# A two-layer graph kernel: the first layer's order written out for each engine by itself, x loaded between the weight slices

## What is computed

```python
h = relu(layernorm(x))                       # x: 1024 x 512, float32
q, k, v = h @ Wq + bq, h @ Wk + bk, h @ Wv + bv
adj = zeros(1024, 1024); adj[src, dst] = 1   # 33,792 edges, sorted by dst
a = q @ k.T / sqrt(512) * adj + (1 - adj) * -1e6
x = x + softmax(a) @ v
h = relu(layernorm(x))
agg = segment_sum(h[src], dst) / max(degree, 1)
out = x + alpha * (agg @ W.T + b)
```

## Time and profile before

| | us |
|---|---|
| median of 3 runs (lowest, highest) | 252.75 (252.17, 253.19) |
| the profiled execution | 252.01 |
| its span, first to last instruction | 250.2 |
| TensorE, VectorE, ScalarE, GpSimd busy | 237.3, 169.9, 79.3, 66.9 |
| mean granted TensorE clock | 0.986 of full |

### The profile page before, as it was taken

The page is one execution under the profiler, slowest core; times in us unless marked ns, Lnnn a source line. Parts: engine busy times, 40 slices in busy tenths (PEclk is TensorE's granted clock), DMA queues, the critical chain, the costliest instruction groups (busy, mean ns, idle before and its releaser), DMA issues.

```text
span 250.2 us, 3366 instructions
## 1 busy us (share of the span) xinstructions
PE 237.3 (95%) x1296; PEld 190.4 (76%) x1296; DVE 169.9 (68%) x352; ACT 79.3 (32%) x139; POOL 66.9 (27%) x102
## 2 busy tenths in 40 slices
PE   7998399949999999999999999999999999999995
PEld 5464388747888887878888888888888888888885
DVE  6998967897999998169584998585856153145322
ACT  2058808834322223013236054141603202041000
POOL 4044312300000000299643156070414503200000
PEclk9999859999999999999999999999999999999999
DMA  6990000000010000100400000000000000001222
GB/s 200 326 355 6 0 0 4 0 0 0 3 42 1 3 0 3 42 1 4 149 19 0 3 0 0 0 3 0 0 0 3 0 0 0 4 3 42 84 102 108
DMA packets 5617, 9.42 MB, mean 38 GB/s; under 512 B 864, under 2 KB 1376, under 8 KB 5600
## 3 DMA queue, kind: packets, MB, share of 16 engines
q1 hardware_dynamic: 4880, 8.91, 10.1%
q10 hardware_dynamic: 720, 0.28, 0.4%
HBM read 7.09 MB, written 2.10 MB: 37 GB/s over the span
## 4 chain that ended last, share of the span: by engine, by line
PE 64%; issue 24%; DVE 4%; ACT 3%; POOL 2%; DMA 2%; SPq 0%; DVEq 0%; POOLq 0%
PE bank L848 14%; PE bank L849 14%; PE bank L850 14%; PE bank L992 12%; PE bank L905 3%; PE bank L1012 3%; PE bank L869 2%; DMA wk_raw<-in_wkT 2%; PE bank L915 1%; DVE g_terms L632 1%; PE bank L929 1%; POOL b_sb L417 1%; DVE ohW L594 1%; ACT h L473 1%; DVE pr L773 1%
## 5 line engine op out<-in xcount | busy, mean ns | idle before, releaser
L594 DVE TENSOR_TENSOR ohW<-iotaW,key_b 128x640 bf16<-128x640 bf16 (+4 forms) x66 | 29.9, 453 | 0.0
L590 DVE TENSOR_TENSOR ohL<-iotaL,lo_b 128x512 bf16<-128x512 bf16 x66 | 27.4, 416 | 1.5 <-issue 1.5
L848 PE MATMUL bank<-V_hi,pT_hi 128*128 128x512 f32 x64 | 25.5, 399 | 0.0
L848 PE MATMUL bank<-hT_hi,GT_hi 128*128 128x512 f32 x64 | 25.0, 391 | 0.0
L849 PE MATMUL bank<-V_lo,pT_hi 128*128 128x512 f32 x64 | 24.9, 390 | 0.0
L850 PE MATMUL bank<-V_hi,pT_lo 128*128 128x512 f32 x64 | 24.9, 390 | 0.0
L850 PE MATMUL bank<-hT_hi,GT_lo 128*128 128x512 f32 x64 | 24.9, 389 | 0.0
L849 PE MATMUL bank<-hT_lo,GT_hi 128*128 128x512 f32 x64 | 24.9, 389 | 0.0
L992 PE MATMUL bank<-A,h_hi 128*128 128x512 f32 x64 | 24.9, 389 | 0.0
L992 PE MATMUL bank<-A,h_lo 128*128 128x512 f32 x64 | 24.9, 389 | 0.0
L869 PE MATMUL bank<-ohW,ohL 128*128 128x160 bf16 (+17 forms) x334 | 23.1, 219 | 0.7 <-DVE ohW L594 0.5
(11 more groups left out here) (135 smaller groups left out, 521.9 us busy)
## 6 DMA issues: line engine op xcount, KB each, us to landing
xs<-in_x SPq DMA_DIRECT2D x4, 512.0 KB, 9.3
out_dram<-o_sb SPq DMA_DIRECT2D x7, 256.0 KB, 2.0
wq_raw<-in_wqT SPq DMA_DIRECT2D x4, 256.0 KB, 5.5
wk_raw<-in_wkT SPq DMA_DIRECT2D x4, 256.0 KB, 6.4
wv_raw<-in_wv SPq DMA_DIRECT2D x1, 1024.0 KB, 11.7
wt_raw<-in_wT SPq DMA_DIRECT2D x1, 1024.0 KB, 5.3
bv_sb<-in_bv SPq DMA_DIRECT2D x1, 256.0 KB, 3.2
b_sb<-in_b SPq DMA_DIRECT2D x1, 256.0 KB, 3.0
```

The source lines that it names most:

```text
L590: nc.vector.tensor_tensor(ohL[:, q % RING, :, :].rearrange("p b (m two) -> p b m two", two=2), bcast(iotaL[:, :].rearrange("p (m two) -> p ...
L594: nc.vector.tensor_tensor(ohW[:, q % RING, :, 0:row].rearrange("p b (m two) -> p b m two", two=2), bcast(iotaW[:, 0:row].rearrange("p (m t ...
L848: mm(out, lhs[0][a], rhs[0][b], start=(first and k == 0), stop=False)
```

## The change

- `PLAN` and the code that makes lists from it go. Three orders stand in their place, one for each engine: `PE_ORDER`, `ACT_ORDER`, `DVE_ORDER`. `cN` is N batches of counts, `oN` N batches of one-hots, `kN` the copy of group N into A, `sq` is `squares`, `dot` is `csum`. GpSimd follows ScalarE's `sum` and `sq`.
- `stats` goes: ScalarE makes the statistics of all eight tiles.
- SP issues the first half of x (tiles 0 to 3) between weight slices 1 and 2.
- `g` leaves the rotation of the banks (it goes to bank 7, with semaphores `g_ps` and `g_kept`), so `PROJ` has 21 entries and V7 has index 20 instead of 21.
- `bb` is a step of its own, on TensorE and VectorE.
- G4's low part waits for `u_sum`, V waits for its tile's `hT_lo`, and SP's load of bv no longer waits for `proj_hi`.

```diff
-PLAN = [(("Mk", 0), [], [], 0),
-        (("Mk", 1), [], [], 5),
-        (("M", 0), ["stats 0", "stats 1"], [], 2),
...
-        (("V", 6), [], [], NB),
-        (("V", 7), [], [], 0)]
+PE_ORDER = ("Mk0 bb Mk1 c4 M0 c3 M1 c2 T0 c2 M2 T1 c2 T2 M3 T3 c5 G0 c1 T4 g G1 c3 T5 T6 c6 G2 T7 G3 c3 G4 G5 c4 G6 u c4 V0 "
+           "c4 V1 c3 G7 c6 V2 c4 V3 c4 V4 V5 c2 V6 V7 c4")
+ACT_ORDER = ("sum0 sum1 sum2 sq0 sum3 sq1 sq2 rows0 rows1 k0 M0 sq3 sum4 M1 T0 rows2 sum5 k1 M2 T1 rows3 T2 k2 M3 T3 sq4 k3 "
+           "sum6 sq5 sum7 rows4 rows5 T4 wv0 sq6 rows6 k4 T5 sq7 G0 T6 G1 rows7 k5 G2 wv1 T7 G3 k6 G4 k7 G5 k8 G6 u k9 V0 "
+           "V1 k10 G7 k11 V2 k12 V3 V4 k13 V5 V6 k14 k15 V7")
+DVE_ORDER = ("o12 bb M0 o2 M1 o1 T0 o2 T1 M2 T2 o1 M3 T3 o1 gsum o2 g T4 o8 T5 T6 o1 wv0 o3 T7 G0 G1 G2 o2 wv1 G3 usum o2 G4 "
+           "o2 G5 o2 G6 o2 dot0 o3 dot1 o2 dot2 o2 u o2 dot3 o4 V0 o1 V1 o3 G7 dot4 o2 dot5 o1 dot6 o1 V2 o1 V3 o1 V4 V5 "
+           "V6 dot7 V7")
...
+PROJ = [s for s in PE_STEPS if s[0] in ("M", "u", "G", "V")]
...
             for k in range(KD):
+                if k == 2:
+                    rows_in(0)
+                    rows_in(1)
                 for raw, w_d, loaded in ((wq_raw, wqT_d, ld_wq), (wk_raw, wkT_d, ld_wk)):
                     sp.dma_start(raw[:, k, :], w_d[k * P:(k + 1) * P, :]).then_inc(loaded[k], 16)
...
+            rows_in(2)
+            rows_in(3)
...
                         if n == 0:
-                            act.wait_ge(proj_lo, proj_index(("g", 0)) + 1)
+                            act.wait_ge(g_kept, 1)
...
+                        if n == KD:
+                            dve.wait_ge(u_sum, 1)
...
+                elif step == "bb":
+                    pe.wait_ge(vec_ready, 1)
+                    mm(bank[7][:, 0:KD + 1], f(ones_r[:, :]), bprod[:, :], start=True, stop=True).then_inc(bb_ps, 1)
+                elif step == "g":
+                    pe.wait_ge(g_sum, 1)
+                    pe.wait_ge(hT_lo, KD)
+                    for m in range(KD):
+                        last = mm(bank[7][:, m:m + 1], t_g[:, m * P:(m + 1) * P], f(ones_r[:, 0:1]), start=True, stop=True)
+                    last.then_inc(g_ps, 1)
...
+                        pe.wait_ge(hT_lo, n + 1)
```

More of the change, by code:

```diff
@@ L85 @@
 LAST = {g: max(t for t in range(ET) if any(p[0] == g for p in pieces(t))) for g in range(NG)}
-PLAN = [(("Mk", 0), [], [], 0),
[22 rows of a table removed]
-        (("V", 6), [], [], NB),
-        (("V", 7), [], [], 0)]
-STATS0 = sum(s.startswith("stats") for _, others, _, _ in PLAN for s in others)
-WARM = 8
[L124 to L147, removed]
@@ new lines, with steps @@
+WARM = 8
+def steps(order):
+    out, at = [], 0
+    for step in order.split():
+        what = step.rstrip("0123456789")
+        n = int(step[len(what):] or 0)
+        if what in ("c", "o"):
+            out.append(("count", at, at + n))
+            at += n
+        else:
+            out.append((what, n))
+    assert at in (0, NB)
+    return out
+PE_STEPS, ACT_STEPS, DVE_STEPS = steps(PE_ORDER), steps(ACT_ORDER), steps(DVE_ORDER)
+PROJ = [s for s in PE_STEPS if s[0] in ("M", "u", "G", "V")]
@@ L394, in norm1 @@
             def norm1(layer, t):
-                pool.wait_ge(stats, layer * STATS0 + t + 1)
+                pool.wait_ge(stats, t + 1)
                 link(nc.gpsimd.tensor_scalar(var_e[:, layer, t:t + 1], mv[:, t, 1:2], EPS, None, ALU.add))
@@ L407, in _ @@
             pool.wait_ge(consts, 5)
[L408 to L411, removed]
+            for step, n in ACT_STEPS:
+                if step == "sum":
                     minus_mean(n)
-                elif step == "squares":
+                elif step == "sq":
                     norm0(n)
@@ L460, in norm_relu @@
                                      scale=rstd[:, layer, t:t + 1]).then_inc(relu, 1)
[L462 to L467, removed]
+            act.wait_ge(consts, 2)
+            nc.scalar.activation(iotaL[:, :], iota_i[:, 0:P], ACT.Copy).then_inc(tables, 1)
+            nc.scalar.activation(iotaW[:, :], iota_i[:, 0:NT * WIN], ACT.Copy, bias=1.0).then_inc(tables, 1)
+            for step, n in ACT_STEPS:
+                if step == "sum":
                     if n % 2 == 0:
@@ L470, in _ @@
                     nc.scalar.activation(h1[:, n, :], xs[:, n, :], ACT.Copy, accum_out=xsum[:, n:n + 1]).then_inc(summed, 1)
-                elif step == "squares":
-                    act.wait_ge(centred, n + 1 - STATS0)
+                elif step == "sq":
+                    act.wait_ge(centred, n + 1 )
                     nc.scalar.activation(h1[:, n, :], xs[:, n, :], ACT.Square, bias=nmean[:, n:n + 1],
@@ L485, in _ @@
                                          ACT.Copy).then_inc(hT_hi, 1)
[L486 to L492, removed]
+                elif step == "k":
+                    act.wait_ge(oh_used, LAST[n] // BATCH + 1)
+                    nc.scalar.activation(A[:, :, n * GRP:(n + 1) * GRP], bank[n % 2][:, :].rearrange("p (h d) -> p h d", h=NT),
+                                         ACT.Copy).then_inc(count_kept, 1)
                 elif step in ("M", "u", "G", "V"):
@@ L611, in split_lo @@
                 nc.vector.tensor_tensor(hl[1][:, :, :], raw[:, :, :], f(hl[0][:, :, :]), ALU.subtract).then_inc(w_lo, 1)
[L613 to L625, removed]
+            edge_keys()
+            dve.wait_ge(ld_bqk, 32)
+            link(nc.vector.tensor_scalar(bqk_s[:, :, :], bqk[:, :, :], SCALE, None, ALU.mult))
+            nc.vector.tensor_tensor(bprod[:, 0:KD], bqk_s[:, 0, :], bqk[:, 1, :], ALU.mult).then_inc(vec_ready, 1)
+            for step, n, *to in DVE_STEPS:
+                if step == "count":
+                    one_hots(n, to[0])
+                elif step == "bb":
+                    dve.wait_ge(bb_ps, 1)
+                    nc.vector.tensor_scalar(flag[:, :], bank[7][:, KD:KD + 1], float(P), None, ALU.is_lt).then_inc(flag_ready, 1)
+                    nc.vector.tensor_scalar(windowed[:, :], bank[7][:, KD:KD + 1], float(P), None, ALU.is_ge)
+                    nc.vector.tensor_reduce(bb[:, :], bank[7][:, 0:KD], AX.X, ALU.add).then_inc(bb_kept, 1)
                 elif step in ("gsum", "usum"):
@@ L649, in _ @@
                 elif step == "g":
-                    i = proj_index((step, n))
-                    dve.wait_ge(proj, i + 1)
-                    nc.vector.tensor_copy(g0[:, :], bank[2 + i % 4][:, 0:KD]).then_inc(proj_lo, 1)
+                    dve.wait_ge(g_ps, 1)
+                    nc.vector.tensor_copy(g0[:, :], bank[7][:, 0:KD]).then_inc(g_kept, 1)
                 elif step == "u":
                     i = proj_index((step, n))
-                    dve.wait_ge(proj_hi, hi_before(i + 1))
+                    dve.wait_ge(proj_hi, i + 1)
                     nc.vector.memset(dbad[:, :], 0.0).then_inc(proj_lo, 1)
-                elif step == "csum":
+                elif step == "dot":
                     dve.wait_ge(relu, n + 1)
-                    dve.wait_ge(proj_hi, hi_before(proj_index(("u", 0)) + 1))
+                    dve.wait_ge(proj_hi, proj_index(("u", 0)) + 1)
                     if n >= 2:
@@ L883, in cols @@
                 return (every, k, slice(m * width, (m + 1) * width))
-            for step, n, *to in STEPS:
+            for step, n, *to in PE_STEPS:
                 if step == "count":
                     count(n, to[0])
+                elif step == "bb":
+                    pe.wait_ge(vec_ready, 1)
[6 more added lines that the diff above has]
+                    last.then_inc(g_ps, 1)
                 elif step == "T":
@@ L917, in _ @@
                     last.then_inc(proj, 1)
-                elif step in ("u", "g", "G", "V"):
+                elif step in ("u", "G", "V"):
                     i = proj_index((step, n))
@@ L925, in _ @@
                         last = mm(ps[:, :], f(ones_r[:, :]), t_u, start=True, stop=True)
-                    elif step == "g":
-                        pe.wait_ge(g_sum, 1)
-                        for m in range(KD):
-                            last = mm(ps[:, m:m + 1], t_g[:, m * P:(m + 1) * P], f(ones_r[:, 0:1]), start=True, stop=True)
                     elif step == "G":
```

26 lines of the change are left out of this document (8 added, 18 removed), and 20 rows, old and new, of the table PLAN.

## The result

| | before | changed |
|---|---|---|
| median, 4 runs each (lowest, highest), us | 252.46 (251.96, 253.19) | 244.61 (243.59, 245.41) |
| ratio, 95% interval | | 0.969 (0.964 to 0.973) |
| the profiled execution, us | 252.01 | 245.40 |
| its span, us | 250.2 | 243.6 |
| mean granted TensorE clock in it | 0.986 | 0.993 |

The forecast was 244.3 us. The four runs of the changed kernel come in two kinds: two took 245.40 and 245.41 (span 243.6, clock 0.993), two 243.81 and 243.59 (spans 242.0 and 241.8, clock 0.999 and 1.000).

A forecast was written before the change was run, and what follows sets the result against it. TensorE's waits and slowed clock in the first layer's front were the time to win, with VectorE nearly full. G0 at 28.1 plus 65.0 put `scores(0)` at 93.1 against 101.47, −8.4 us: forecast 244.3 us, range 242.3 to 247.3.

The forecast's parts named there:

- the layout's own 243.6: Whole kernel: time expected for an execution like the profiled 252.01 us one, after −8.4 us, before adding 0.74 us.
- The start: `bb` between `Mk0` and `Mk1`: new TensorE wait of 1.1 us, `Mk1` from 9.8, VectorE waiting about 1 us at `o5`.
- Term 1: Front up to G0: VectorE sets G0, which starts at 28.1 instead of 32.91 us; −4.8 us.
- ScalarE's statistics at no cost: Before T0: 2.6 us added on ScalarE, seven statistics and two normalisations done by 15; cost nothing, cover 4 us.
- The loads: x ahead of weight slices 2 and 3: slice 3 lands near 12.5, M0 wants it at 14.3; hidden, 1.8 us spare.
- Term 2: G0 to `scores(0)`, 68.56 us before: clock and waits gained, `g`, one-hot waits and a V7 wait added; −3.55 us.
- The stretch behind: Behind `scores(0)`: nothing changes, the old length of 148.7 us stays within 0.3.
- a clock of 1.00 throughout the first layer: Sign to look for: TensorE's granted clock at 1.00 in the whole first layer; 0.5 in the front would refute.
- the rival that I gave 0.13: TensorE's clock falls at a remaining stall, costing about 2.7 us, so 247.0 us; chance 0.13.
- loads: Start of the kernel: bias loads and slice 3 may slip by 2 us under x's load, about 245.8 us; chance 0.10.
- VectorE as a bound by 3.5 us: VectorE, without a gap, holds TensorE at most counts: 5% more on 70 us, 247.8 us; chance 0.06.
- slower: Slice 3 queues behind everything, M0 blocks the counts and the clock falls; landing at 22 gives 254.7 us; chance 0.03.

The follow-up runs named there:

- all three repairs: Changed kernel with V7 copied out before the last two groups of counts, `bb` behind `Mk1` and tile 6's squares earlier; 241.20 us, ratio 0.953.
- the first experiment: Changed kernel with ScalarE copying V7 out before the last two groups of counts (V7 k14 k15); 242.33 us, ratio 0.959.
- VectorE work: Changed kernel with two bn_stats and two bn_aggr, results unused, put back on VectorE behind the seventh one-hot pair; 246.01 us, ratio 0.973.

## Why the prediction was right

The time lay 0.3 us from the forecast, and the mechanism was in the main the forecast one. That the distance is so small is partly luck: no run took 244.6 us. The two runs at full clock took 243.81 and 243.59, which is the layout's own 243.6, without the 0.74 us that I added because the old median lay above the old profiled run; the fall of the clock in the other two, which I had left to a rival, lifted the median by about as much. By the steps of the prediction:

- **The start.** `bb` starts at 9.73 and `Mk1` at 9.98 (forecast 9.8), `o5` waits 1.04 us for the first count (forecast about 1). The run with `bb` late shows that this costs 0.84 us up to the end. The trace puts only 0.53 us down as idle in front of `bb`, while the distance from start to start gives 9.73 − 5.12 − 3.55 = 1.06. In this profile one of the 16 records of `Mk0` and `Mk1` is missing, as in that of x late, which shows 0.63. The five other profiles with `bb` early show 0.93 to 0.95 us at this place, and that with the 0.13 that the overlap hides is the distance.
- **Term 1, −4.8 us to G0.** Measured −4.69 (28.22 for 28.1), with `hT_lo` as the releaser and 0.75 us of TensorE idle (forecast 0.8). Its parts are shown one by one, counted from `bprod`: `gsum` 2.76, the statistics on ScalarE 1.58, x's place 2.06, and `bb` −0.84. They don't add up to 4.69, and need not: each was undone alone in the new order.
- **ScalarE's statistics at no cost.** Right with x early, though the seven statistics and two normalisations end at 16.2 and not by 15: the first copy of A behind them, at 16.60, still waited 0.40 us for TensorE. But the cover was judged by the wrong waiter. I named T0, 4 us away. The run with x late moved the statistics by 3.4 us and G0 by 2.1, through the copy of A that stands behind them.
- **The loads.** M0 didn't wait, and VectorE didn't wait for the small loads of the biases (bq's took 4.8 us for 4.3 before). x landed for a first sum at 9.87, at the late end of my 8 to 10, and the sum of tile 2, from the second load, started at 11.24. In the run of all three repairs M0 did wait, so the 1.8 us that I had to spare are not safe once TensorE comes earlier.
- **Term 2, −3.55 us.** The stretch from G0 to `scores(0)` took 65.13 us, forecast 65.0. That is luck in part, as two entries in it were wrong and nearly cancelled: I had 0.7 us of TensorE waiting for one-hots, and the trace has none; and I took T6's old wait of 0.26 off, and the trace has one of 1.07 us. The row of tile 6 waits for three operations of GpSimd behind its squares, and one of them took 1.29 us where 0.19 is its short value; the prediction gives them no length. Why no matmul waits for one-hots stays open: the wait for tile 6 didn't remove those waits, for the run with its squares early has neither. The new wait in front of `scores(0)` was 1.90 us, forecast 2.05, and its larger cause was the forecast one: the first experiment removed 1.25 of it by ScalarE's order alone.
- **The stretch behind** was forecast at 148.7 within 0.3 us. Without a fall of the clock it is 148.55 to 148.64, by the six profiles that have none there; with one it is 150.25, so in the profiled run this sign failed, and so did the one of a clock of 1.00 throughout the first layer. This is the rival that I gave 0.13: it is half true, as two of four runs have it. I priced it at 2.7 us, from the old fall; measured 1.7. The size was off because the old fall lasted from about 29.5 to 36.3 us and this one 3.4 us, from about 94.8 to 98.2. The other rivals (loads, VectorE as a bound by 3.5 us, slower) did not come.

The clock by stall, over the runs of this study; a mean clock of 0.993 is read as one fall. Four kernels have `bb` early, the 1.90 us in front of `scores(0)` and nothing longer: the changed kernel, x late, tile 6 early, VectorE work. In them 8 of 16 runs show 0.993, and the others 0.999 or 1.000. The runs with `gsum` or `usum` early have the 1.90 us and one longer wait (3.50 and 2.56); 7 of 8 show a fall or more. The three profiles that caught a fall near the 1.90 us (changed kernel, `gsum` early, `usum` early) have it begin within 1.5 us of the end of that wait. The 2.56 us themselves caused none in their profile. In the two kernels with 0.65 us there, none of 9 runs has one. But in the run with `bb` late, with the same 1.90 us, none of 4 does either; with four runs that may be chance. So that V7's place on ScalarE took the falls away is likely, not shown.

The Trainium skill, "TensorE: Matmul & The Clock Gate", Part 1, calls the window over which activity is judged free-running. The 8 of 16 agree: the same stall, at the same place of the program, is met in some executions and not in others.

## What to carry to other kernels

Lay a new order out by distances from start to start of the old trace, one engine at a time, and look for the instruction that ends each wait: here that gave the start of a stage within 0.3 us after 90. When one engine (here VectorE) has almost no gap left, work on it costs its full length: 2.76 us for `gsum`'s 2.75, and 1.58 for statistics of 1.61, and what can be moved behind the instruction that another engine waits for is worth as much. A short wait of another engine then costs what it makes the full one stand: TensorE's waits before `bb` and before T6 cost 0.84 and 0.86 us, and with them went 0.83 and 0.80 us of VectorE's waits. At the seam of two stages look at the in-order engine between producer and consumer: a copy that nobody waited for stood in front of the one that TensorE needed, and cost 1.25 us and, likely, in half of the runs the clock.

## What the runs showed of the hardware

GpSimd's operations on a 128x1 tile have no fixed length. `var_e` takes 0.19 us at 27.31 and 39.75 in the changed kernel, and 1.29 at 34.72, where the operation behind it starts 1.37 us later; `nmr` takes 0.19 and at worst 1.49 (at 19.57). The place in the program matters: the run with `bb` late has the same 1.29 us, 1.1 us earlier. VectorE's one-hots are not enough to explain it. They run without a gap during the long operation at 34.72, but also during the short one at 39.75, and in the run with tile 6's squares early during the 0.30 us at 32.62:

```profile
34.74 0.48 DVE L550 TENSOR_TENSOR ohW<-iotaW,key_b 128x640 bf16<-128x640 bf16 x1
35.14 0.41 DVE L546 TENSOR_TENSOR ohL<-iotaL,lo_b 128x512 bf16<-128x512 bf16 x1
35.48 0.48 DVE L550 TENSOR_TENSOR ohW<-iotaW,key_b 128x640 bf16<-128x640 bf16 x1
35.94 0.42 DVE L546 TENSOR_TENSOR ohL<-iotaL,lo_b 128x512 bf16<-128x512 bf16 x1
...
39.38 0.48 DVE L550 TENSOR_TENSOR ohW<-iotaW,key_b 128x640 bf16<-128x640 bf16 x1
39.78 0.43 DVE L546 TENSOR_TENSOR ohL<-iotaL,lo_b 128x512 bf16<-128x512 bf16 x1
```

Between 35.48 and 35.94 VectorE takes 0.46 us where its other distances of that pair are 0.40, just as GpSimd's operation ends (36.01). That looks as if the two held each other up, but it proves nothing: the run with tile 6's squares early has 0.48 us at the same step (35.99 to 36.47), and GpSimd does nothing there. Why `var_e` is long stays open. The Trainium skill, "SBUF — State Buffer", section "SBUF: two separate sides", says that the two share a port pair under an exclusive lock and that the loser blocks, for VectorE operations with two SBUF inputs against GpSimd ones that read SBUF. Both kinds meet at 34.72 and at 39.75, with 1.29 and 0.19 us, so this trace neither bears the rule out nor refutes it; no run took VectorE's work away from under the long one.

A fall of the clock may follow 1.9 us of idling (8 of 16 runs), and need not follow 3.50 (one of four runs with that wait has a mean clock of 1.000). In the changed kernel it lasts about 3.4 us and costs 1.7, where the one of the old kernel lasted 6.8.
